# Context attention: two or three zero products on TensorE in front of each row step

## The reference

```python
def _L0_xattn_ref(query, key, value, mask, Wq, bq, Wk, bk, Wv, bv, Wo, bo):
    q = proj(query, Wq, bq)
    k = proj(key, Wk, bk)
    v = proj(value, Wv, bv)
    scores = jnp.einsum('bhqd,bhkd->bhqk', q, k) / np.sqrt(D_K)
    scores = jnp.where(m == 0, jnp.float32(-1000000000.0), scores)
    p_attn = jax.nn.softmax(scores, axis=-1)
    x = jnp.einsum('bhqk,bhkd->bhqd', p_attn, v)
    ...
    return x @ Wo.T + bo
```

## Time and profile before

| | us |
|---|---|
| median of 3 runs | 2968.14 |
| lowest, highest | 2961.43, 2969.96 |
| the profiled execution's own time | 2965.02 |
| its span | 2963.1 |
| PE busy (share of the span) | 2423.0 (82%) |
| DVE busy | 1625.7 (55%) |
| ACT busy | 1130.8 (38%) |
| POOL busy | 1009.9 (34%) |
| granted clock of TensorE, mean | 0.878 |

### The profile page before, as it was taken

One profiled execution on the slowest core, in us unless ns is written; L12 is line 12 of the kernel. 1 busy time (PEld: TensorE's weight loads), 2 busy tenths in 40 slices (PEclk: granted clock), 3 DMA queues, 4 the chain that ended last, 5 costly groups with the idle time before them and its releaser, 6 DMA issues. The chain is left out here.

```text
span 2963.1 us, 46030 instructions
## 1 busy us (share of the span) xinstructions
PE 2423.0 (82%) x15970; PEld 1294.9 (44%) x15970; DVE 1625.7 (55%) x2578; ACT 1130.8 (38%) x2043; POOL 1009.9 (34%) x878
## 2 busy tenths in 40 slices
PE   3848997674998797899999998867739999848996
PEld 2613334323887574233333332732612222247885
DVE  2758873556332333566666663245748999552223
ACT  1515664332000332344444444223516777711121
POOL 1841002511222012577777766231650000003331
PEclk7959998555999898899999999865959999968998
DMA  5442212423564666122222221543451111024555
GB/s 128 93 95 60 60 35 61 93 74 110 159 200 159 197 194 176 58 71 78 83 86 76 86 83 35 156 81 80 102 107 35 39 50 34 9 86 146 198 196 175
DMA packets 251787, 299.63 MB, mean 101 GB/s; under 512 B 64973, under 2 KB 197739, under 8 KB 251115
## 3 DMA queue, kind: packets, MB, share of 16 engines
q1 hardware_dynamic: 219978, 226.15, 25.6%
q0 software_dynamic: 27616, 67.97, 9.0%
q10 hardware_dynamic: 4032, 3.41, 0.8%
HBM read 205.49 MB, written 91.25 MB: 100 GB/s over the span
## 5 line engine op out<-in xcount | busy, mean ns | idle before, releaser
L1590 ACT ACTIVATE a_probs<-a_cols 128x512 f32<-128x512 f32 (+3 forms) x896 | 445.2, 549 | 245.5 <-PE a_cols L1521 168.1
L1611 DVE TENSOR_REDUCE a_mxw<-a_rows 128x2 f32<-128x1024 f32 (+1 forms) x448 | 475.7, 1099 | 75.1 <-PE a_rows L1479 46.9
L2037 DVE TENSOR_REDUCE a_mxw<-a_rows 128x2 f32<-128x1024 f32 x256 | 313.3, 1224 | 208.4 <-PE a_rows L1875 206.7
L2015 ACT ACTIVATE a_probs<-a_cols 128x1024 f32<-128x1024 f32 x256 | 261.7, 1024 | 267.5 <-PE a_cols L1904 248.8
L1856 POOL TENSOR_TENSOR a_sums<-a_sums,a_probs 128x1024 f32<-128x1024 f32 x128 | 309.6, 2419 | 99.2 <-ACT a_probs L2015 86.5
L1521 PE MATMUL a_cols<-a_qs,a_ks 50*128 50x512 bf16 (+7 forms) x1792 | 279.4, 368 | 15.9 <-DMA a_qs<-a_nparts 9.6
L2291 PE MATMUL e_psU<-e_xT,e_w 128*128 128x256 f32 x1216 | 274.1, 384 | 1.9 <-ACT e_xT L2338 1.2
L531 PE MATMUL t_psP<-t_xT,t_wf 128*128 128x256 f32 x1024 | 238.3, 391 | 37.4 <-ACT t_xT L624 16.7
L1900 PE MATMUL a_cols<-a_qf,a_kf 64*128 64x512 f32 x1024 | 266.8, 599 | 0.0
L1479 PE MATMUL a_rows<-a_ks,a_qs 48*128 48x512 bf16 (+3 forms) x896 | 175.9, 389 | 110.6 <-DMA a_ks<-k_scratch 67.6
L1549 PE MATMUL a_out<-a_probs,a_vs 128*17 128x256 f32 (+4 forms) x3328 | 259.2, 385 | 0.2 <-ACT a_probs L1590 0.2
(11 more groups left out here) (244 smaller groups left out, 3077.9 us busy)
## 6 DMA issues: line engine op xcount, KB each, us to landing
e_w<-in_w SPq DMA_DIRECT2D x69, 512.0 KB
e_w<-in_w SPq DMA_DIRECT2D x30, 1024.0 KB
a_qs<-q_scratch SPq DMA_DIRECT2D x336, 64.0 KB, 2.3
qk_wide_scratch<-t_f SPq DMA_DIRECT2D x32, 512.0 KB, 2.9
q_scratch<-t_parts POOLq DMA_DIRECT2D x128, 96.0 KB, 2.4
a_ks<-k_scratch SPq DMA_DIRECT2D x144, 64.0 KB, 2.4
vw_scratch<-t_v SPq DMA_DIRECT2D x16, 520.0 KB, 5.7
a_vs<-vw_scratch SPq DMA_DIRECT2D x16, 520.0 KB, 6.1
```

The lines of the kernel that those rows point to most:

```text
L1590: act.activation(pr[ug % RING][:, 2 * hp + e, c0:512], psC[(2 * at + e) % 3][:, 0:512 - c0], ACT.Exp, scale=scale).then_inc(ex_done, 1)
L1611: dve.tensor_reduce(mxw[w][:, a, :, hp, t % 4:t % 4 + 1], src[:, :, 0:n], AX.X, ALU.max).then_inc(s_free, 1)
L2015: act.activation(pr[i][:], psC[i % 2][:], ACT.Exp, scale=scale).then_inc(ex_done, 1)
L2037: dve.tensor_reduce(mxw[:, j % 2, :, j // 2:j // 2 + 1], psR[:], AX.X, ALU.max).then_inc(s_free, 1)
```

## The change

In `rows_step`, between the wait for the bank and the step's own products, TensorE issues zero products into the first half of the bank that the step is about to overwrite: three for even j, two for odd j. Steps 0 to 6, which run before the first column step, are left as they are. So steps 7 to 31 have them: 2 + 6 x (3 + 2 + 3 + 2) = 62 zero products in each of the two stages. Nothing else changes.

```diff
                     if j == 0:
                         pe.wait_ge(main_ld[p], 16 * n_ld * (g // 4 + 1))
                     bank_free(("step", g, j))
+                    if 4 * g + j >= AHEAD:
+                        zero_products(pe, G, dst[:, 0, :], 3 - j % 2)
                     for t in range(QT // 2):
                         for e in range(2):
                             mm = pe.matmul(dst[:, e, t * SC:(t + 1) * SC], qs[p][ROWS_K[e], 0, w, m, t * P:(t + 1) * P],
```

## The result

The changed kernel takes **2982.24 us** (median of 8 runs, 2977.69 to 2991.82) against 2961.06 us (median of 8, 2959.96 to 2969.96) before: 21 us more, ratio 1.0072, interval (95%) 1.0053 to 1.009. The forecast was 2989 us, 21 us above the median of 3 known when it was made (2968.14).

A forecast was written before the change was run, and what follows sets the result against it. Both stages were taken as bound at half clock by the placement's wait and TensorE's own work. 2/3 x 38 - 1/3 x 12 = +21 us on 2968 gave 2989 us, range 2954 to 3010.

The forecast's parts named there:

- leg 1: Part of a group's period from transpose to the next group's columns: 6.40 us, set by SyncE's placement, TensorE waiting 1.48.
- leg 2: Part of a group's period from columns to next transpose: TensorE's work alone, 4.37 us before, 3.26 at full clock with zeros.
- All at half clock, +38 us: Both stages never leaving half clock: zeros cost 26.5 us each, less filled waits, 20.2 in a1 and 17.7 in a4.
- The drain: Last zero product of a row step finishing before the next product: counted as nothing, some 0.2 us a step in the range.
- The wait for VectorE in a4: TensorE's one 6.3 us wait in a4, behind GpSimd's bias addition: claimed to swallow five zeros, 2.1 us.
- Which level: Whether granted clock in both stages stays half or rises: expected to rise in some groups, giving +21 us in sum.
- about a third of the steps: Estimated share of row steps in both stages at full clock, weighting the sum 2/3 x 38 - 1/3 x 12.
- seldom to outlive the next placement: Full clock, once reached in a group, would mostly fall at the reopened wait before the columns, 1.6 to 2.8 us.
- 1.1 us less a group: At full clock a group's period is 9.66 us instead of 10.77; -12 us over 12 groups of both stages.
- Never rising: Rival: the clock stays at half in both stages; 3006 us, up to 3016 with the whole drain; chance 0.23.
- Rising and staying: Rival: the clock rises in the first group or two and holds across placement waits; -12 us or slightly more, 2955; chance 0.13.

The follow-up runs named there:

- the three profiles: The changed kernel, unaltered, profiled in three executions: spans 2989.7, 2981.9 and 2974.4 us, against 2963.1 for the kernel before.
- the 48-row kernel: The changed kernel with its 62 zero products a stage on 48 of 128 array rows: 2992.09 us against 2965.39 before the change, ratio 1.0097.
- the wait filled: The changed kernel plus eight zero products before each group's wait for placed maxima: 2967.15 us against 2965.39 before the change, ratio 1.0009.

## Why the prediction was right

- **What bounds the stages** (leg 1 with the placement's wait, leg 2 of TensorE's work alone, both at half clock): held. At half clock the zeros filled the wait and lengthened leg 2 by 2.56 us, for 2.13 forecast.
- **All at half clock, +38 us:** the line through the three profiles gives +39. The periods give some +42, an estimate: the 48-row kernel, at half clock throughout, has 96.4 + 99.7 = 196.1 us of columns, and eleven periods of the change are 0.9 us longer, 206 against 163.6. Two parts were off, in opposite ways. The drain, which I took as nothing and kept as "some 0.2 us" a step in the range, is 0.25 us, half of it in front of the zeros, for which I had no term, and the period at half clock is 14.1 us for some 13.6. The wait for VectorE in a4 shrank from 6.32 to 2.14 us, where I counted 2.1 us of it as filled: that period takes 16.3 us before and after, so its ten zeros were free.
- **Which level:** "about a third of the steps" at full clock was 14, 27 and 39% of the columns' time in three profiles (27 of 195 us, 51 of 189, 72 of 184), 27% as a mean. It rises in some groups and falls mostly at the placement's wait: of 16 such waits that began at full clock in the three profiles, 10 were followed by half clock (1.75 to 2.89 us) and 6 weren't (0.74 to 1.75 us), so "seldom to outlive the next placement" was too strong. One more fall came behind a wait of 1.64 us for queries. With the wait filled and the same zeros in the steps, the clock is at 1.00 through a1.
- **The term that was mis-sized: "1.1 us less a group" at full clock, -12 us.** At full clock, with the change's zeros, a group gains nothing. The third profile of the change has one group at full clock from end to end, and one in which leg 2 is:

```profile
586.48:596.62 10.14, 8.03 (x78) 2.38 (x75) 8.25 (x16) 4.48 (x9) 4.62 (x6) 1.00 0.35 92
```

```profile
609.17 0.40 PE L1111 MATMUL a_rows<-g_ident,a_mx 128*32 128x128 f32 x1
...
615.63 0.41 PE L1131 MATMUL a_cols<-a_qs,g_ctx_keys 51*77 51x512 bf16 x2 [1.39 <-issue]
...
619.52 0.28 PE L1111 MATMUL a_rows<-g_ident,a_mx 128*32 128x128 f32 x1
```

The periods are 10.14 and 10.35 us, for 9.66 forecast. Leg 1 is 6.46, as forecast (6.40), but leg 2 is 3.89, not 3.26: the drain was left out here too, and TensorE's own work doesn't halve (the eight products of a row step take 0.25 us to the next product, 0.37 at half clock). And the group of the earlier trace rows, with 10.77 us, is one of the two longest of a1; from the second to the seventh transpose (565.37 to 616.18) the five periods average 10.2. Held at full clock by the filled wait, the columns of a1 take 75.5 us from first to last against 78.6 before, and a4's more than before (91.3 against 85.0, with the two falls there). In the sum this term had a weight of a third, 4 us.
- **The number is in part luck.** With some +42 us at half clock, 27% at full clock and nothing gained there, the sum would be 0.73 x 42 = +31 us. The columns of the three profiles take 32, 26 and 20 us more than before. The forecast's +21 matches the medians to a microsecond, closer than its terms are.
- **The rivals.** Never rising is what one zero a step, or 48 rows, gave (+16 and +27 us). Rising and staying, priced at 2955, never came with the change's own zeros; where the clock stayed up with more of them, in the steps or in the wait, there was no gain (+15 and +2 us).
- **The Trainium skill** ("TensorE: Matmul & The Clock Gate", section "Why this matters for your kernels"), by its first half, would have the 48-row kernel, with TensorE busy 77.36 of 78 us, at full clock; the trace disagrees (0.50). By its second half idle gaps lose the clock; the trace agrees (1.91 us of waiting, then half clock).

## What to carry to other kernels

A stage that TensorE fills by time but not by rows and columns can sit at half clock for its whole length. Zeros that lift it are paid in full wherever they stand on the path, and at half clock twice (0.427 us for 0.215); put them in front of a wait that TensorE has anyway, and enough of them that little of the wait is left. Look first at what the faster engine will then wait for: here the placement took back whatever leg 1 gained. And compare stages, not spans, where executions differ elsewhere (here by up to 9 us).

## What the runs showed of the hardware

- With TensorE busy 99% of 78 us on products that fill the array in part (48 to 51 rows by 77 or 128 columns, the kernel's own ones in pairs side by side; 77 rows by 17 columns; one of 128 by 32 a group), the granted clock stayed at 0.50. Zero products of the same length and number on 128 rows and 128 columns, or as pairs of 64 rows side by side in their place, raised it.
- Products on all 128 rows between products on 64-row halves start 0.13 us late, and the next one 0.12 us late, at half clock. As two products of 64 rows side by side they start on time (0.43 us behind the pair before them).
- Products of nothing but zeros raise the clock.
- In the profiles of the change, placement waits of 1.76 to 2.9 us at full clock were each followed by its fall, waits of 0.74 to 1.39 us weren't, and 1.75 us was once and once wasn't. With fourteen zeros in the wait the clock also fell once behind waits of at most 0.81 us.
